# Splitting the edge layer's broadcast loads by partitions, and making the next step's hot matrices ahead of an addition

## The reference, cut to what matters

```python
def _L2_gnn_ref(h, e, src, dst, W1, b1, W2, b2):
    x = jnp.concatenate([h[src], h[dst], e], axis=1)
    m = jax.nn.relu(x @ W1 + b1) @ W2 + b2
    return jax.ops.segment_sum(m, dst, num_segments=h.shape[0])
```

## Time and profile before

| | us |
|---|---|
| median of 3 runs | 4026.42 |
| the three runs | 3996.96, 4028.32, 4026.42 |
| the profiled execution | 4006.19 |
| its span | 4004.5 |
| PE busy in the span | 3278.3 (82%) |
| DVE busy | 2217.2 (55%) |
| POOL busy | 1251.6 (31%) |
| ACT busy | 1012.2 (25%) |
| edge layer, from POOL's first gather to its last | 2199.3 to 3491 |

### The profile page before, as it was taken

One profiled execution on the slowest core, in us unless ns is written; L12 is line 12 of the kernel. 1 busy time (PEld: TensorE's weight loads), 2 busy tenths in 40 slices (PEclk: granted clock), 3 DMA queues, 4 the chain that ended last, 5 costly groups with the idle time before them and its releaser, 6 DMA issues.

```text
span 4004.5 us, 127161 instructions
## 1 busy us (share of the span) xinstructions
PE 3278.3 (82%) x56384; PEld 3016.0 (75%) x56384; DVE 2217.2 (55%) x2894; ACT 1012.2 (25%) x2184; POOL 1251.6 (31%) x1252
## 2 busy tenths in 40 slices
PE   0768999999996888898886577777767776789998
PEld 0757999999996888888886366666656565689898
DVE  8974777666767766677767244434544454431122
ACT  0025777777771000000000111111111111110000
POOL 5587000000002010121211665666655555501100
PEclk9977999999996999999997677777877777799999
DMA  4315777777776999998885343443333333379797
GB/s 122 99 38 179 277 282 281 274 270 270 282 284 236 377 382 380 389 364 351 349 341 212 86 113 105 109 114 107 115 107 103 105 111 107 94 281 343 297 375 322
DMA packets 285690, 904.35 MB, mean 226 GB/s; under 512 B 97944, under 2 KB 162702, under 8 KB 256850
## 3 DMA queue, kind: packets, MB, share of 16 engines
q1 hardware_dynamic: 235802, 857.37, 55.5%
q0 software_dynamic: 35520, 36.44, 6.7%
q10 hardware_dynamic: 13832, 2.70, 0.4%
HBM read 644.17 MB, written 252.83 MB: 224 GB/s over the span
## 4 chain that ended last, share of the span: by engine, by line
PE 38%; issue 37%; DVE 10%; DMA 6%; POOL 4%; POOLq 2%; DVEq 2%; SPq 1%; another core or an unknown queue 0%; ACT 0%; ACTq 0%
PE ps L1642 10%; PE ps L1459 8%; PE ps L1454 5%; DMA stream<-a_weights 5%; PE ps L1673 4%; PE ps L1637 4%; PE ps L1676 3%; PE ps L1562 2%; POOL wend L909 2%; POOL stream L916 2%; DVE operand_room L2300 1%; DVE junk L1780 1%; DVE operand_room L2318 1%; DVEq L2326 1%; DMA table<-node_room 1%
## 5 line engine op out<-in xcount | busy, mean ns | idle before, releaser
L936 POOL DMA_INDIRECT stream<-table,stream x660 | 792.2, 1200 | 527.0 <-PE ps L1642 307.4
L1411 PE MATMUL ps<-operand_room 64*128 64x50 bf16 (+1 forms) x18750 | 646.1, 222 | 49.0 <-DVE operand_room L2023 18.8
L1411 PEld LDWEIGHTS ps<-operand_room 64*128 64x128 bf16 x18750 | 618.8, 163 | 80.3 <-issue 28.5
L1459 PE MATMUL ps<-stream,node_room 125*64 125x125 f32 x10000 | 581.5, 278 | 56.9 <-DMA stream<-a_weights 47.7
L1459 PEld LDWEIGHTS ps<-stream,node_room 125*64 125x64 f32 x10000 | 559.5, 141 | 67.4 <-DMA stream<-a_weights 53.7
L1115 ACT CAST stream<-ps 128x500 bf16<-128x500 f32 (+2 forms) x700 | 431.2, 633 | 243.6 <-PE ps L1411 197.1
L1115 ACT COPY stream<-ps 128x500 f32<-128x500 f32 (+2 forms) x700 | 422.5, 620 | 0.0
L1256 ACT ACTIVATE node_room<-ps 128x320 f32<-128x320 f32 x300 | 131.3, 438 | 895.1 <-remote 448.6
L1454 PE MATMUL ps<-operand_room,stream 125*125 125x192 bf16 x3750 | 320.4, 247 | 4.4 <-POOLq L578 4.4
L1454 PEld LDWEIGHTS ps<-operand_room,stream 125*125 125x125 bf16 x3750 | 314.8, 137 | 4.7 <-POOLq L578 4.7
L2383 DVE TENSOR_TENSOR node_room<-slot_f,stream 128x625 f32<-128x625 f32 x240 | 184.0, 810 | 184.9 <-remote 146.6
(11 more groups left out here) (293 smaller groups left out, 4574.1 us busy)
## 6 DMA issues: line engine op xcount, KB each, us to landing
stream<-a_weights SPq DMA_DIRECT2D x100, 3125.0 KB, 14.8
a_weights<-stream SPq DMA_DIRECT2D x500, 312.5 KB
stream<-a_counts SPq DMA_DIRECT2D x100, 1562.5 KB, 9.1
a_counts<-stream SPq DMA_DIRECT2D x500, 156.2 KB
stream<-sorted_edges SPq DMA_DIRECT2D x80, 781.2 KB
node_room<-sorted_edges SPq DMA_DIRECT2D x40, 781.2 KB
stream<-dst_run SPq DMA_DIRECT2D x20, 1031.2 KB
stream<-table,stream POOLq DMA_INDIRECT x660
```

What stands on the lines that cost most here:

```text
L936: pool.indirect_dma_start(emsg[s][:, t, :], None, tables[L2][:, :], bass.IndirectOffsetOnAxis(src_t[j % 3][:, at:at + 1], 0))\
L1411: ins = pe.matmul(out if step == 0 else out[:, 1:2], low[s][rows_a, :, t], planes[s][rows_a, t // TI, what, :, t % TI], start=step == 0, s ...
L1459: ins = pe.matmul(ps_sum[SUM_BANK[MATRIX[k]][b]][half:half + D, 0:Q], tab_in_of(k)[0:Q, h, :], a[0:Q, h, :], start=h < 2, stop=h >= NPP - 2)
```

## The change

The broadcasts of the target runs and of `hot_q`'s first row are each issued as two DMAs, to partitions 0 to 111 and 112 to 124; the broadcast for `hot_p` goes to all 128 partitions in one DMA, the last three of which nobody reads. The semaphore counts follow: 48 in place of 32 for each target run, and one more increment of 16 for each piece of a unit. In DVE's step, `arrive(c)` moves from behind `slots_of(c+1)` to behind `unit_hots(c+1)`.

```diff
-    LOADS = [sum(3 + (h == 0 and lo == 0) for b, h, lo, hi in now) for now in PIECES]
+    LOADS = [sum(4 + (h == 0 and lo == 0) for b, h, lo, hi in now) for now in PIECES]
...
-                        sp.dma_start(dst_bc[i % 2][0:Q, :], dst_run[bass.ds(start, RUN)].partition_broadcast(Q))\
-                          .then_inc(bc_in, 16)
+                        for a, z in ((0, EVEN), (EVEN, Q)):
+                            sp.dma_start(dst_bc[i % 2][a:z, :], dst_run[bass.ds(start, RUN)].partition_broadcast(z - a))\
+                              .then_inc(bc_in, 16)
...
-                    for tile, i in ((hot_q, 0), (hot_p, 1)):
-                        sp.dma_start(tile[u % HRING][0:Q, place].rearrange("p (s r) -> p s r", r=P),
-                                     rows_of(b, h)[i, lo:hi, :].partition_broadcast(Q)).then_inc(unit_in[u % HRING], 16)
+                    for tile, i, a, z in ((hot_q, 0, 0, EVEN), (hot_q, 0, EVEN, Q), (hot_p, 1, 0, P)):
+                        sp.dma_start(tile[u % HRING][a:z, place].rearrange("p (s r) -> p s r", r=P),
+                                     rows_of(b, h)[i, lo:hi, :].partition_broadcast(z - a))\
+                          .then_inc(unit_in[u % HRING], 16)
...
-                    v.wait_ge(bc_in, 32 * (i + 1))
+                    v.wait_ge(bc_in, 48 * (i + 1))
...
                     if 0 <= c + 1 < NCH:
                         slots_of(c + 1)
-                    if 0 <= c < NCH:
-                        arrive(c)
                     if c + 1 == 0:
                         dst_half(GROUPS - 1, "linear")
                         v.wait_ge(qparts_rdy, GT)
                         split_sources(0)
                     if 0 <= c + 1 < NCH:
                         unit_hots(c + 1)
                     if c + 1 == 0:
                         split_sources(1)
                         v.wait_ge(tab_out, 16 * GROUPS)
                         v.wait_ge(qparts_rdy, GROUPS)
+                    if 0 <= c < NCH:
+                        arrive(c)
```

## The result

The changed kernel takes 4032.28 us (median of 15 runs, 4021.28 to 4044.01), the kernel before 4010.62 (median of 15, 3960.04 to 4030.37). The ratio is estimated at 1.0074, with an interval of 1.0051 to 1.0096 (the two medians alone give 1.0054): slower, by 0.5 to 1.0%. The profiled execution has 4027.86 us and a span of 4026.1, where before had 4006.19 and 4004.5.

The account below looks back on a forecast made before the run. In the edge layer no engine was full; POOL's gathers plus PE's release set each step. Start -18 us, steady loads 0, reordering 0: 3988 from the profiled 4006.2, 4008 from the median; predicted 4003, range 3970 to 4040.

Parts of the forecast that it names:

- The start: Edge layer's start: table piece lands sooner, POOL's first gather 27 us earlier, `s_done` of step 0 at 2249: 18 us gained.
- The DMA rate: Broadcasts: split over more engines, from 131 GB/s at share 0.32 to close to 418 GB/s; lower end 131.
- Steady steps, the loads: Edge layer's steady steps: faster broadcasts save nothing, taken as 0; gain bounded under 8 us in 60 steps.
- Rival 2: Steady steps: broadcasts on all 16 engines slow PE by 1.2 us a step, 72 us, total 4080; chance 0.08.
- rival 3: Layer's start gains nothing, as POOL's earlier gathers make PE creep: 4006 by profiled run, 4020 by median; chance 0.17.
- rival 4: Broadcasts: the split doesn't spread the load, DMA share stays at 0.32, total 4020; chance 0.05.
- Rival 1: Steady steps gain too: each gives back the tail behind POOL's last gather, some 2 us, 120 us, about 3890; chance 0.08.
- The reordering: DVE's steady step: `unit_hots` ahead, `arrive` 2.1 us later, taken as 0, bounds -9 to +21 us.
- the cover of the moved pieces: Steady steps: ACT's in-order wait for PE's units hides the later `arrive`; gone at most once in a group.
- neither term of a step: Steady step: lasts POOL's eleven gathers plus PE's few us to release POOL (5.66 and 8.31); neither in the diff.
- The 4003: Whole kernel's predicted time in us: between 3988 from the profiled run and 4008 from the median, nearer the median.
- 0.12 of 0.62: Chances: own case has 0.62; within it 0.12 for being faster, as 18 us off the low run is 3979.

Follow-up runs that it names:

- e1: All broadcasts split, `arrive` left in its old place, against the kernel before: 3988.56 us, 0.9947 at the slow level; 3625.51 us, 0.9864 at the fast.
- e3: Only the first two target runs and units split, `arrive` left in its old place, against the kernel before: 3992.57 us, 0.9972.
- e4: Only the first two target runs and units split, with `arrive` moved, against the kernel before: 4036.54 us, 1.0066.
- e2: Only `arrive` moved, loads as before, against the kernel before: 4054.84 us, 1.0114 at the slow level; 3680.99 us, 1.0007 at the fast.
- x1: e1 with `unit_hots` made ahead of `slots_of`; against the kernel before, fast level only: 3637.53 us, 0.9881, and 3638.41 us, 0.9891.
- x3: e1 with both hot matrices multiplied by one once more; against the kernel before, fast level only: 3672.83 us, 0.9989, later 1.0003 and 0.9993.
- x2: e1 with the addition `arrive` ahead of `slots_of`, against the kernel before: 3601.61 us, 0.9791 at the fast level; 4090.31 us, 1.0197 at the slow.

## Why the prediction was wrong

1. **The start: right in sum, partly by luck.** The forecast was 18 us; between the layer's first broadcast issue and the sixth step's first gather the profiled executions differ by 17.5 (the same stretch is 22, 21 and 22 us shorter than before in e1, e3 and e4), and e3, which has the start alone, has a median 20 us lower, though its interval just touches 1. The terms were less exact. The table's piece was to land within 6 us; POOL was released 11.3 us after its issue (2159.47 to 2170.77). Reckoned from the layer's start POOL's first gather came 21.2 us earlier (28.5 less the 7.2 of chance), where I had 27. Its 44 gathers ended at 2234.4, 63.6 us after the first began; I had 62. PE was better off than I thought: `s_done` of step 0 released DVE at 2221.22, when POOL was still gathering, and not near 2249. So POOL never stood before its fifth step, as it did for 9.30 us, but before its sixth, for 15.63. The earlier release and the longer wait offset each other.
2. **The DMA rate: right in kind, too high in size.** The share went from 0.32 to 1.02 in the first burst, and SP's 6.24 us are gone; but with all engines busy the broadcasts move 246 GB/s, not close to 418. At that rate 2.66 MB take an estimated 10.8 us, where I had 6.5, which by this estimate is most of why the table's piece came later than forecast. The Trainium skill ("DMA: Bandwidth & Descriptors", rules for kernel authors) says of two halves by partitions that they serialize, because both use all 16 engines. Here the whole used 5, and e1, which splits it into 112 and 13 partitions, is faster: 0.9947 at the slow level and 0.9864 at the fast one. So the rule's reason isn't met in this case, and its advice doesn't carry over, as the prediction had argued.
3. **Steady steps, the loads: right at the slow level.** 0 forecast; e1 less e3 is 4 us. Rival 2 is refuted by e1, rival 3 by e1's gain of 24 us, rival 4 by the share of 1.02. Rival 1's tail behind POOL's last gather did not shrink: POOL's idle time is 5.79 us in e1, 5.58 before.
4. **The reordering: this is the step that failed.** "I take 0; bounds from the length of the moved pieces [...] -9 to +21 us." It costs 43 us alone, twice the upper bound; in the profiled steps 0.6 us (the change less e1), 0.9 (e4 less e3) and 1.3 (e2 less before). The sentence ahead of it, that the cover of the moved pieces is ACT's in-order wait, was right: nobody waited for the addition. What I had left out is that a move of DVE's work needs no semaphore to reach PE. I had both halves in hand: the profile showed gathers of 2.18 us beside DVE and PE creeping while POOL gathers, and I wrote that neither term of a step was in the diff. Both were: by the traces DVE's order sets which gathers are slow, and PE's free time ends earlier when the first four are through earlier. That the order costs is shown by e2 and e4; that it costs by this way is read from the traces and no run isolates it. The prediction's own sign of being wrong, a steady step whose length changes by over half a microsecond, is what happened (0.78 us). I applied the first half to the start of the layer and to nothing else.
5. **The rivals lacked this case.** The slower one had a DMA cause. None had a cost without a wait.
6. **The base and the chances.** The 4003 stood on a median of 4026.42 us from three runs; fifteen gave 4010.62, so the base was 16 us high. And 0.12 of 0.62 is 0.07, where the sum of the chances for faster has 0.06.

**What stays open.** Why PE creeps beside indirect DMAs, why from about the fifth gather on, and why some sets don't have it. The creeping goes on in stretches without broadcasts, so they aren't the cause. Whether PE's free time follows the end of DVE's work or POOL's count of gathers no run has told apart: x1 and x3, made for that, met only the fast level. The kept traces speak for the gathers. The fourth gather of a step ends 7.2, 7.2 and 7.1 us after the first one's start in before, e1 and e3, and 6.8 us in the four kernels in which the addition was moved; DVE is busy for 1.1 to 1.2 of the 2 us from 6 to 8 us in the first six of these seven, and for 0.44 in x2, where PE begins 19 products and not more or fewer than in the other moved ones (18 to 20). One more candidate, PE's instruction stream, leaves no mark in the DMA records. In 2400 to 2800 us the larger of the two queues named instruction shows these packets, MB and share, before at the slow level and then the changed kernel at the fast one:

```profile
q8 instruction: 37, 0.61, 0.8%
```

```profile
q8 instruction: 50, 0.82, 0.9%
```

That is an estimated 1.4 and 1.2 us for a packet, one for each 125 products or so, while the pauses come after every four or five. And x2's extra loss beyond 8 us has no explanation here.

**The version to keep.** e1, the split without the move, beats both kernels at the slow level (0.9947 against 1.0074). At the fast level x2 is the best (0.9791 to 0.9825 in four sets; e1 0.9864), but at the slow one it is the worst, 1.0197. e1 is faster than before at both.

## What to carry to other kernels

A reordering that no semaphore notices can still cost: before it is costed at nothing, look at which instructions of other engines get longer beside the moved work (here POOL's gathers, 0.95 us alone and 1.9 to 2.4 beside it), not only at who waits for it. Where one engine's rate depends on another's activity, a step is priced by how much work the first gets done inside the other's stretch. A part that is clearly right and a part that is thought neutral belong in two kernels, since the gain of one hid half of the loss of the other.

## What the runs showed that I had not expected

- The same kernel has two levels by set of runs: 4011 and 3679 us, with 3465 and 4102 products in the first 400 us. In one set the kernel before lay between 3972.6 and 4042.04, in another between 3643.25 and 3702.8. A ratio measured at one level doesn't carry to the other: the order alone is 1.0114 and 1.0007, the addition first 1.0197 and 0.98.
- At the slow level PE starts four or five products and then pauses about 1 us, again and again, from 6 us after the first gather of a step on (33 products in 2 us, then 18, 12, 9, 6), and it stays slow until some us after the last.
- POOL's indirect DMA takes 0.95 us while DVE does nothing (324 of the 660 in the kernel before, 0.947 to 0.961). Beside other work of DVE it takes longer by what that work is, by the means of e1 and e2: 1.9 us beside the comparisons of `unit_hots`, 2.1 to 2.4 beside the additions of `slots_of`, 1.1 to 1.2 beside those of `unit_slot_hots`. The Trainium skill ("SBUF — State Buffer", the trap that DVE blocks DMA) has such a case with a factor of five; here it is at most 2.5 by these means.
- DMA spread over all 16 engines isn't DMA at the highest rate: the broadcasts move 246 GB/s at a share of 1.02, the dense stage's loads 418 at 0.98.
